# One attention and expert kernel: the step order of all five engines is written anew

## The reference, cut to what matters

```python
# layer 0; 16 heads, sequence length 64
x = rms_norm(h, ln_in_w)
mixed = where(vm, x @ v_qkv, x @ l_qkv)              # expert by token
q, k, v = split(mixed); q, k = apply_rotary(q, k)
h = h + where(vm, sdpa(q, k, v, causal) @ v_dense, ... @ l_dense)
cq = rms_norm(h, ln_post_cross_w) @ cq_w; ck, cv = split(ctx @ ckv_w)
h = h + sdpa(cq, ck, cv) @ cdense_w                   # cross attention
mi = rms_norm(h, ln_post_attn_w)
h = h + where(vm, (silu(mi @ v_gate) * (mi @ v_up)) @ v_down, ... l ...)
# layer 1
mp = ctx @ W_mem.T; a = softmax(h @ mp.T / 16); mc = a @ mp
gate = sigmoid(concat(h, mc) @ W_gate + b_gate)
out = rmsnorm(h + gate * mc, norm_w)
```

## Time and profile before

| | us |
|---|---|
| median of 3 runs | 484.67 |
| lowest, highest | 483.89, 485.15 |
| profiled execution, its own time | 484.13 |
| its span, first to last instruction | 482.3 |
| PE busy | 432.3 (90%) |
| DVE busy | 356.2 (74%) |
| ACT busy | 247.4 (51%) |
| POOL busy | 130.4 (27%) |

### The profile page before, as it was taken

The page is one execution under the profiler, slowest core; times in us unless marked ns, Lnnn a source line. Parts: engine busy times, 40 slices in busy tenths (PEclk is TensorE's granted clock), DMA queues, the critical chain, the costliest instruction groups (busy, mean ns, idle before and its releaser), DMA issues. The chain is left out here.

```text
span 482.3 us, 10858 instructions
## 1 busy us (share of the span) xinstructions
PE 432.3 (90%) x3844; PEld 335.6 (70%) x3844; DVE 356.2 (74%) x810; ACT 247.4 (51%) x706; POOL 130.4 (27%) x246
## 2 busy tenths in 40 slices
...
PEclk9999999999599999999999999999999999999997
...
GB/s 236 259 43 92 204 110 140 209 211 195 95 99 46 1 101 33 34 35 97 37 23 99 46 2 107 27 34 35 23 12 71 96 23 23 66 64 69 65 45 65
DMA packets 27315, 39.44 MB, mean 82 GB/s; under 512 B 3969, under 2 KB 21377, under 8 KB 27265
## 3 DMA queue, kind: packets, MB, share of 16 engines
...
...
## 5 line engine op out<-in xcount | busy, mean ns | idle before, releaser
L863 ACT ACTIVATE th<-b_ps,mrh 128x256 f32<-128x256 f32 (+1 forms) x45 | 20.2, 449 | 59.5 <-PE b_ps L1656 59.5
L1142 DVE TENSOR_REDUCE mx<-xyz 128x8 f32<-128x512 f32 x64 | 43.7, 683 | 8.8 <-PE xyz L1499 8.8
L1144 DVE TENSOR_TENSOR E<-xyz,mx 128x512 f32<-128x512 f32 x64 | 44.2, 691 | 2.2
L1499 PE MATMUL xyz<-kT,qT 32*64 32x128 f32 (+1 forms) x768 | 42.5, 320 | 2.1 <-PE xyz L1499 0.2
L1526 PE MATMUL xyz<-cst,E 128*128 128x128 f32 x256 | 36.4, 279 | 6.4 <-ACT E L827 4.7
L259 POOL TENSOR_TENSOR qk<-E 128x256 f32<-128x256 f32 x16 | 14.2, 890 | 93.0 <-DVE E L1124 93.0
L1653 PE MATMUL b_ps<-w_gu_hi,ms_hi 128*128 (+2 forms) x90 | 36.7, 409 | 2.2 <-DVE hid L1228 1.6
L1540 PEld LDWEIGHTS xyz<-vb,kT 128*64 128x64 f32 x1024 | 33.7, 143 | 6.9 <-issue 5.1
L1526 PEld LDWEIGHTS xyz<-cst,E 128*128 128x128 f32 x256 | 28.2, 141 | 14.1 <-ACT E L827 8.1
L1540 PE MATMUL xyz<-vb,kT 128*64 128x18 f32 (+1 forms) x1024 | 37.0, 222 | 0.9 <-DVE kT L1152 0.5
L1653 PE MATMUL b_ps<-w_gu_lo,ms_hi 128*128 (+2 forms) x90 | 33.3, 371 | 0.0
...
...
## 6 DMA issues: line engine op xcount, KB each, us to landing
...
xm<-h_rows SPq DMA_DIRECT2D x17, 128.0 KB, 2.1
h_rows<-xm SPq DMA_DIRECT2D x17, 128.0 KB, 1.7
...
out_dram<-over_gu_lo SPq DMA_DIRECT2D x16, 128.0 KB, 1.7
xq<-x_rows SPq DMA_DIRECT2D x13, 128.0 KB, 3.1
...
ctxT_a<-in_ctxT_dram SPq DMA_DIRECT2D x8, 128.0 KB, 2.3
```

Source lines behind the costliest of these rows:

```text
L863: act.activation(th[i % 2][:, 0:w], m_banks(m)[j % 2][:, 0:w], ACT.Tanh, scale=mrh[:, m % 2:m % 2 + 1]).then_inc(S["th_ready"], 1)
L1142: dve.tensor_reduce(mx[:, t, heads], s, AX.X, ALU.max).then_inc(max_ready, 1)
L1144: dve.tensor_tensor(E[t][:, b * 512:(b + 1) * 512].rearrange("p (h k) -> p h k", k=SEQ), s, mx[:, t, heads].unsqueeze(2).to_broadcast([P, ...
L1499: last = pe.matmul(xy[t][q, hp, o:o + w], qT[t][rows, c, q], kT[t][rows, (2 * c + b) * w:(2 * c + b + 1) * w], start=not masked, stop=True ...
```

## The change

Only the table `ORDER` is different. Every engine does the same steps, as often as before; their order is another one on all five engines, written out with regard to the time that TensorE takes to change between shapes of operations. No function, no wait inside a step and no buffer is touched, and no step moves from one stage to another. Stages W2, W3, W5 and W6 have the same edits as W4 with other numbers. The order of `score_a`/`score`, `pv` and `cpv` also changes in W0; L1's list is also new. Of W1, W7 and MID the lists of PE stand here, of W1 SP's too.

```diff
             ("W4", dict(
                 sp="""
-    m_in:4 m_in:5 load_ca:10 load_x:10 m_out:4 m_out:5""",
+    m_in:4 m_in:5 m_out:4 load_x:10 load_ca:10 m_out:5""",
                 act="""
-    qkT:8 m_sq:4 qkT:9 miT:4 gu0:4 score:8 gu1:4 score:9 probT:8 probT:9 gu2:4 hT0:4 ctxT:8 hT1:4
-    ctxT:9 h1T:8 dense:8 cproj:8 miT:5 dense:9 m_sq:5 h1T:9 gu0:5 cproj:9 cscore:8 gu1:5 cprobT:8
-    hT0:5 gu2:5 cscore:9 rope:10 hT1:5 cprobT:9 cctxT:8 cctxT:9 rope:11""",
+    qkT:8 qkT:9 m_sq:4 miT:4 score:8 gu0:4 probT:8 score:9 gu1:4 probT:9 gu2:4 hT0:4 m_sq:5 hT1:4
+    ctxT:8 miT:5 ctxT:9 dense:8 h1T:8 cproj:8 dense:9 gu0:5 h1T:9 cproj:9 gu1:5 cscore:8 gu2:5
+    cprobT:8 cscore:9 hT0:5 cprobT:9 hT1:5 rope:10 rope:11 cctxT:8 cctxT:9""",
                 dve="""
-    qkT:8 qkT:9 miT:4 score:8 score:9 probT:8 gu0:4 probT:9 gu1:4 pv:8 gu2:4 pv:9 ctxT:8 hT0:4 hT1:4
-    dense:8 ctxT:9 dense:9 miT:5 down:4 cscore:8 gu0:5 gu1:5 cprobT:8 cscore:9 gu2:5 hT0:5 cprobT:9
-    hT1:5 rope:10 down:5 cpv:8 cpv:9 rope:11 cdense:8 cdense:9""",
+    qkT:8 qkT:9 score:8 miT:4 score:9 gu0:4 gu1:4 probT:8 probT:9 gu2:4 hT0:4 pv:8 pv:9 hT1:4 ctxT:8
+    dense:8 ctxT:9 miT:5 down:4 dense:9 gu0:5 cscore:8 gu1:5 cscore:9 gu2:5 cprobT:8 hT0:5 cprobT:9
+    hT1:5 cpv:8 rope:10 cpv:9 rope:11 cdense:8 down:5 cdense:9""",
                 pool="""
-    m_sq:4 sort:6 sort:7 get:10 get:11 dense:8 dense:9 m_sq:5 rope:10 rope:11""",
+    m_sq:4 get:10 sort:6 sort:7 m_sq:5 get:11 dense:8 dense:9 rope:10 rope:11""",
                 pe="""
-    qkT:8 qkT:9 miT:4 score_a:8 score:8 score_a:9 score:9 gu0:4 gu1:4 probT:8 probT:9 pv:8 gu2:4 pv:9
-    hT0:4 ctxT:8 hT1:4 ctxT:9 dense:8 down:4 h1T:8 dense:9 cproj:8 miT:5 cscore_a:8 h1T:9 cscore:8
-    gu0:5 cproj:9 gu1:5 cprobT:8 cscore_a:9 cscore:9 hT0:5 gu2:5 cpv:8 cprobT:9 hT1:5 down:5 cpv:9
-    cctxT:8 cctxT:9 cdense:8 cdense:9""",
+    qkT:8 qkT:9 score_a:8 score:8 score_a:9 miT:4 score:9 gu0:4 probT:8 gu1:4 probT:9 gu2:4 hT0:4 pv:8
+    pv:9 hT1:4 ctxT:8 ctxT:9 miT:5 dense:8 down:4 h1T:8 dense:9 cproj:8 gu0:5 cscore_a:8 h1T:9
+    cscore:8 cproj:9 gu1:5 cscore_a:9 cscore:9 gu2:5 cprobT:8 hT0:5 cprobT:9 hT1:5 cpv:8 cpv:9 cctxT:8
+    down:5 cctxT:9 cdense:8 cdense:9""",
             )),
...
             ("W1", dict(
                 sp="""
-    load_w:10 q_in:11 q_in:12 load_w:11 q_st:13 load_w:12 q_in:13 load_w:14 q_st:14 load_w:13 q_in:14
-    q_st:15 load_w:15 q_st:16 load_w:17 q_in:15 load_w:16 q_in:16 q_st:17 load_wb:0 q_st:18 q_st:19
-    q_st:20 load_w:18 load_ca:4 load_w:19 load_x:4""",
+    load_w:10 q_in:11 q_in:12 load_wb:0 q_st:13 load_w:12 q_in:13 q_in:14 q_st:14 load_w:11 q_in:15
+    q_st:15 load_w:14 q_in:16 q_st:16 load_w:13 load_w:15 load_x:4 q_st:17 load_w:17 load_w:16 q_st:18
+    q_st:19 q_st:20 load_w:18 load_w:19 load_ca:4""",
                 act="""
...
+    q_sq:9 q_sq:10 sort:0 q_sq:11 q_sq:12 q_sq:13 sort:1 q_sq:14 q_sq:15 dense:2 q_sq:16 dense:3 get:4
     get:5 rope:4 rope:5""",
                 pe="""
-    qkT:2 q_T:9 qkT:3 score_a:2 score:2 q_qk:13 q_v:13 score_a:3 probT:2 q_T:10 score:3 pv:2 q_v:14
-    ctxT:2 q_T:11 q_qk:14 q_v:15 dense:2 q_qk:15 q_T:12 probT:3 q_v:16 pv:3 q_qk:16 q_T:13 h1T:2
-    ctxT:3 cproj:2 q_v:17 q_qk:17 q_T:14 dense:3 q_v:18 cscore_a:2 q_T:15 cscore:2 q_qk:18 q_v:19
-    h1T:3 q_qk:19 q_T:16 cproj:3 q_qk:20 q_v:20 cscore_a:3 cscore:3 cprobT:2 cprobT:3 cpv:2 cpv:3
-    cctxT:2 cdense:2 cctxT:3 cdense:3 fold:0""",
+    qkT:2 q_T:9 qkT:3 score_a:2 q_v:13 score:2 score_a:3 q_T:10 q_qk:13 probT:2 q_v:14 q_T:11 score:3
+    pv:2 q_v:15 q_qk:14 probT:3 ctxT:2 q_T:12 q_qk:15 dense:2 q_v:16 pv:3 q_T:13 q_qk:16 ctxT:3 h1T:2
+    q_v:17 dense:3 q_qk:17 cproj:2 q_T:14 h1T:3 cscore_a:2 q_v:18 q_qk:18 q_T:15 cscore:2 cproj:3
+    q_v:19 q_qk:19 cscore_a:3 q_T:16 cscore:3 q_qk:20 q_v:20 cprobT:2 cpv:2 cprobT:3 cctxT:2 fold:0
+    cpv:3 cctxT:3 cdense:2 cdense:3""",
...
-    m_sq:10 sort:12 sort:13 dense:14 dense:15 m_sq:11""",
+    m_sq:10 sort:12 m_sq:11 dense:14 dense:15 sort:13""",
                 pe="""
-    qkT:14 qkT:15 miT:10 score_a:14 score:14 score_a:15 score:15 gu0:10 probT:14 gu1:10 probT:15 pv:14
-    gu2:10 ctxT:14 pv:15 hT0:10 ctxT:15 dense:14 dense:15 h1T:14 hT1:10 down:10 cproj:14 miT:11 h1T:15
-    cscore_a:14 cproj:15 cscore:14 gu0:11 gu1:11 cscore_a:15 cscore:15 hT0:11 cprobT:14 gu2:11
-    cprobT:15 cpv:14 hT1:11 down:11 cctxT:14 cpv:15 cctxT:15 cdense:14 cdense:15""",
+    qkT:14 qkT:15 score_a:14 score:14 score_a:15 miT:10 score:15 gu0:10 probT:14 gu1:10 probT:15 pv:14
+    gu2:10 hT0:10 ctxT:14 pv:15 dense:14 hT1:10 down:10 h1T:14 ctxT:15 miT:11 cproj:14 dense:15
+    cscore_a:14 cscore:14 h1T:15 gu0:11 gu1:11 cproj:15 cprobT:14 cscore_a:15 cscore:15 gu2:11 hT0:11
+    cpv:14 cprobT:15 hT1:11 down:11 cctxT:14 cpv:15 cctxT:15 cdense:14 cdense:15""",
             )),
...
     sort:14 sort:15 m_sq:12 m_sq:13 m_sq:14 m_sq:15 m_sq:16""",
                 pe="""
-    miT:12 gu0:12 gu1:12 gu2:12 hT0:12 mem:0 hT1:12 down:12 miT:13 miT:14 gu0:13 gu1:13 gu2:13 gu0:14
-    miT:15 hT0:13 hT1:13 gu1:14 gu2:14 down:13 gu0:15 hT0:14 hT1:14 gu1:15 gu2:15 down:14 miT:16
-    hT0:15 hT1:15 gu0:16 gu1:16 down:15 gu2:16 hT0:16 mem:1 hT1:16 down:16 mem:2 mem:3 mem:4 mem:5
+    miT:12 gu0:12 gu1:12 gu2:12 hT0:12 mem:0 mem:1 hT1:12 down:12 miT:13 miT:14 gu0:13 gu1:13 gu2:13
+    gu0:14 miT:15 hT0:13 hT1:13 gu1:14 down:13 hT0:14 gu2:14 gu0:15 gu1:15 hT1:14 down:14 miT:16
+    gu2:15 hT0:15 gu0:16 hT1:15 gu1:16 gu2:16 down:15 hT0:16 hT1:16 mem:2 down:16 mem:3 mem:4 mem:5
     mem:6 mem:7""",
             )),
```

More of the change, by code:

```diff
@@ L419, in xattn_kernel @@
-                    cproj:3 q_out:20 wsplit:17 cprobT:2 cscore:3 cprobT:3 wsplit:18 wsplit:19 cctxT:2 rope:4 cctxT:3
-                    fold:0 rope:5""",
-                dve="""
[L422 to L426, removed]
+                    q_sq:9 qkT:2 q_T:9 wsplit:6 qkT:3 wsplit:7 wsplit:8 wsplit:9 q_T:10 score:2 q_sq:10 wsplit:10
@@ L448, in xattn_kernel @@
+                    dense:4 ctxT:5 miT:1 down:0 dense:5 gu0:1 cscore:4 gu1:1 cscore:5 gu2:1 cprobT:4 hT0:1 cprobT:5
+                    hT1:1 cpv:4 rope:6 cpv:5 rope:7 cdense:4 down:1 cdense:5""",
                 pool="""
-                    m_sq:0 sort:2 sort:3 get:6 get:7 dense:4 dense:5 m_sq:1 rope:6 rope:7""",
+                    m_sq:0 get:6 sort:2 sort:3 m_sq:1 get:7 dense:4 dense:5 rope:6 rope:7""",
                 pe="""
-                    qkT:4 qkT:5 miT:0 score_a:4 score:4 score_a:5 score:5 gu0:0 gu1:0 probT:4 probT:5 pv:4 gu2:0 pv:5
@@ L452, in xattn_kernel @@
-                    hT0:0 ctxT:4 hT1:0 ctxT:5 dense:4 down:0 h1T:4 dense:5 cproj:4 miT:1 cscore_a:4 h1T:5 cscore:4
-                    gu0:1 cproj:5 gu1:1 cprobT:4 cscore_a:5 cscore:5 hT0:1 gu2:1 cpv:4 cprobT:5 hT1:1 down:1 cpv:5
-                    cctxT:4 cctxT:5 cdense:4 cdense:5""",
+                    qkT:4 qkT:5 score_a:4 score:4 score_a:5 miT:0 score:5 gu0:0 probT:4 gu1:0 probT:5 gu2:0 hT0:0 pv:4
+                    pv:5 hT1:0 ctxT:4 ctxT:5 miT:1 dense:4 down:0 h1T:4 dense:5 cproj:4 gu0:1 cscore_a:4 h1T:5
@@ L455, in xattn_kernel @@
+                    cscore:4 cproj:5 gu1:1 cscore_a:5 cscore:5 gu2:1 cprobT:4 hT0:1 cprobT:5 hT1:1 cpv:4 cpv:5 cctxT:4
+                    down:1 cctxT:5 cdense:4 cdense:5""",
             )),
@@ L471, in xattn_kernel @@
-                    hT0:2 ctxT:6 hT1:2 ctxT:7 dense:6 down:2 h1T:6 dense:7 cproj:6 miT:3 cscore_a:6 h1T:7 cscore:6
-                    gu0:3 cproj:7 gu1:3 cprobT:6 cscore_a:7 cscore:7 hT0:3 gu2:3 cpv:6 cprobT:7 hT1:3 down:3 cpv:7
-                    cctxT:6 cctxT:7 cdense:6 cdense:7""",
+                    qkT:6 qkT:7 score_a:6 score:6 score_a:7 miT:2 score:7 gu0:2 probT:6 gu1:2 probT:7 gu2:2 hT0:2 pv:6
+                    pv:7 hT1:2 ctxT:6 ctxT:7 miT:3 dense:6 down:2 h1T:6 dense:7 cproj:6 gu0:3 cscore_a:6 h1T:7
@@ L474, in xattn_kernel @@
+                    cscore:6 cproj:7 gu1:3 cscore_a:7 cscore:7 gu2:3 cprobT:6 hT0:3 cprobT:7 hT1:3 cpv:6 cpv:7 cctxT:6
+                    down:3 cctxT:7 cdense:6 cdense:7""",
             )),
@@ L509, in xattn_kernel @@
-                    gu2:6 pv:11 hT0:6 ctxT:10 hT1:6 ctxT:11 dense:10 down:6 h1T:10 dense:11 cproj:10 miT:7 cscore_a:10
-                    h1T:11 cscore:10 gu0:7 cproj:11 gu1:7 cprobT:10 cscore_a:11 cscore:11 hT0:7 gu2:7 cpv:10 cprobT:11
-                    hT1:7 down:7 cpv:11 cctxT:10 cctxT:11 cdense:10 cdense:11""",
+                    qkT:10 qkT:11 score_a:10 score:10 score_a:11 miT:6 score:11 gu0:6 probT:10 gu1:6 probT:11 gu2:6
+                    hT0:6 pv:10 pv:11 hT1:6 ctxT:10 ctxT:11 miT:7 dense:10 down:6 h1T:10 dense:11 cproj:10 gu0:7
```

193 lines of the change are left out of this document (100 added, 93 removed).

## The result

The changed kernel takes 476.96 us (median of 6, 476.33 to 479.14); the kernel before took 484.35 beside it (median of 6). The ratio is 0.9857, with a 95% interval of 0.9842 to 0.9871. So it is 7.4 us faster, where 12.3 were forecast; the time lies inside the range of 466 to 482. The profiled execution took 476.63 us with a span of 474.8, that is 7.5 under the span before.

What follows compares the result with a forecast made beforehand. PE's queue was taken as the bound, DVE not far behind. Savings of 7.0 (W2 to W6), 0.8 (W7), 1.0 (W1's end) and 3.5 (clock) summed to 12.3 us, giving 472.4 us, range 466 to 482.

Steps and rivals of the forecast that it cites:

- Two signs of being wrong: In W2 to W6: a stretch of 40 us or more, or slices of lower clock, would show the prediction wrong.
- no slice with a 5 in the clock: Sign of being right: the profile after has no slice whose granted clock reads 5, where one read 0.52 before.
- my walk: One stretch of W2 to W6, stepped through the new lists: 3.35 us saved, 1.45 of new waits, net 1.9.
- discount: W2 to W6: 1.4 us a stretch taken instead of 1.9, since the walk on the old lists missed 0.7 of waiting.
- The new waits: In a stretch: 0.4 us at gu0's fifth product, 0.45 more at cprobT:9, 0.3 at ctxT:8, small ones 0.3; sum 1.45.
- The change of shapes: PE's array shape changes cost 0.12 us each; 124 instead of 129 in all, worth 0.6 us in the whole kernel.
- SP: Later m_out:5 delays m_in:6, landing 0.5 us before miT:6 reads it; without that cover, at most about 1 us a stretch lost.
- The end of W1: End of W1: q_qk:20, q_v:20, cprobT:2 and cpv:2 fill cprobT:3's waits of 1.29 and 0.60 us; 1.0 us saved.
- The clock: Behind W1's end: with the hole filled, no fall of the granted clock from 121.3 to 131.9 us; 3.5 us saved.
- the fall stays or moves: Rival: the clock's fall behind W1's end remains or shifts, the other gains happen; 476 us, chance 0.25.
- the walk is right as it stands: Rival, more than forecast: W2 to W6 save 1.9 us each and W1 gives 3; 467 us, chance 0.08.
- slower, by the clock: Rival: stretches without large products bring clock falls of 3.5 to 4 us in each of five stretches; 496 us, chance 0.09.

Runs made afterwards that it cites:

- d2_pv_split: Changed kernel with, in W2 to W6, hT0 between the two pv and hT1 between the two cpv on PE and DVE: 481.99 us, ratio 0.9953.
- d3_mit_back: Changed kernel with, in W2 to W6, PE doing miT of the even tile directly behind qkT again: 493.19 us, ratio 1.0181.
- s1_stretches_only: Kernel before with the new lists in W2 to W6 alone: 478.91 us, ratio 0.9888.
- s4_rope_first: Changed kernel with old W0 and MID; in W1, cctxT:3 before rope:4 on ACT, both ropes before the last two weight splittings on DVE: 474.38 us, ratio 0.9790.
- f1_hole_filled: Kernel before with seven unread products added on PE in the two holes before cprobT:3 at the end of W1: 485.74 us, ratio 1.0021.
- d1_down_back: Changed kernel with, in W2 to W6, the odd tile's down before both cpv again on PE and DVE: 496.03 us, ratio 1.0209.
- d4_down_back_filled: d1_down_back with one unread product ahead of each cctxT in W2 to W6: 496.72 us, ratio 0.9502, on a chip where the kernel before takes 522.

## Why the prediction was right in part and wrong in part

| term | forecast | measured |
|---|---|---|
| W2 to W6, five times | 7.0 | 9.25 (7.40 in W3 to W6, times 5/4) |
| W7 | 0.8 | 1.3 |
| end of W1 and the clock there | 4.5 | 0.25 (W1 and W2 2.10 shorter, less one stretch of 1.85) |
| W0 | 0 | -1.45 |
| MID | 0 | -1.8 |
| L1 | 0 | 0 |
| sum | 12.3 | 7.55 |

The measured time is inside the range, and the forecast of 12.3 us was too large by 4.8 by the table. Two signs of being wrong that the prediction had named came all the same, both in W2, which takes 41.55 us and has a slice of lower clock (the 12th, an 8). The third, a wait of L1629 for the transfer of xm, came once, with 0.48 us in W6. The sign "no slice with a 5 in the clock" came true too and told nothing, since the three falls were spread over slices that read 8.

*The stretch* was right, and its size was between my walk (1.9 us) and its discount (1.4): 1.85. The discount, taken because the walk missed 0.7 us of the old stretch, was not needed. Its steps by the two timelines of W4: `probT` saved 0.67 (0.4 forecast), `cproj:8` with `miT:5` 0.46 (0.6), the start, `qkT`, 0.65 (0.9), the end about 1.0 (0.8 and the shapes). The new waits were at their places: 0.23 at the fifth product of `gu0:4` (0.4), and 0.4 more than before around `cprobT:9` (0.45). The change of shapes was priced too high, at 0.12 each for about 0.06; `d2_pv_split` shows that keeping `hT0` before `pv` is worth more as a cover for DVE's copy than as two changes fewer.

*SP* was right as a danger, and larger than the 1 us I gave it: 1.7 to 2.8 us where the cover is taken away (`d3_mit_back`, and W7 of `s1_stretches_only`). The moves of `down:5` and `miT:4` are one move, and I had priced them as two.

*The end of W1* failed. The step "`q_qk:20` and `q_v:20` stand between `cscore:3` and `cprobT:3`" fills the hole, but it was priced as work moved at no cost. They are the last qkv products: `q_v:20` begins at 117.56 (39.3 us into W1) instead of 114.90 (38.2), and their store releases the gather that ACT's `rope:4` waits for, issued at 121.65 instead of 119.34. I had named this queue only for later gathers with 10 us in hand; here there was none. ACT's wait holds the copy that `cdense:3` needs (1.84 us). DVE does `rope:4` at 127.02, where the kernel before has it at 127.04; in the changed kernel it follows the splitting of weights without idle time, so on DVE the list and not the gather sets it. `s4_rope_first` moves both and takes 0.87 us off W1. The term stays near zero by another comparison as well: W1 and W2 are 0.63 us shorter than in `s1_stretches_only`, which has the old W1.

*The clock* failed, in the way of the rival "the fall stays or moves", priced at 476. The measured 476.96 is next to that, partly by chance, since W0 and MID lost 3.2 us that the rival did not have and the stretches gained 2.3 more. "With the hole filled, I expect no fall there" took one hole for the cause. `f1_hole_filled` shows that without it the fall comes 9 us later, behind the wait of 1.24 us for DVE, and that full clock before that wait was worth nothing (ratio 1.0021). (Another of the rivals has a slip in its sum: "the walk is right as it stands" gives 484.7 less 16.8, that is 468, not 467.)

*W0* was taken as 0 with bounds of 2. In the new list `qkT:1` on ACT stands behind `q_out:4` and `rope:1`, which wait for POOL's scale, and `score_a:1` waits 2.38 us for it instead of 0.64; a fall from 36.2 to 39.7 follows. On the chips where the kernel before takes 484 us all five traces with the new list have this fall, and W0 takes 71.5 to 72.9 us; of the five with the old list none has it, four take 70.5 to 71.7, and `s4_rope_first` 73.6 with a fall at 69.4. So the loss is the list's, though its size of 1.45 is known to half a microsecond at best. *MID* was taken as "the sum is the same work"; it has a fall right at its start (about 1 us), and 0.3 to 1.0 us more without one. The fall is not the list's: it comes at the start of MID in three of seven traces with the new list and in two of seven with the old one, `s1_stretches_only` among them.

*The rival "slower, by the clock"* (496) did not come, but it lay close: `d1_down_back`, with one step put back on two engines, has a fall in each stretch and 496.03 us. That this is the rival's number is chance: it had 3.5 to 4 us for each fall, and `d4_down_back_filled` leaves 1.2 for the clock and 2.7 for waiting. What keeps the clock in the new stretches is that PE has no long wait there. `down` covers one such wait, worth much more than the 0.8 us of my sum; where another opens (`d3_mit_back`), falls come with `down` in place.
